# Attention: a new order of each row's work on TensorE, ScalarE and VectorE, group norm folded into two weights, and one head's key halves added on VectorE

## The reference, cut to what matters

```
xn = scale * x + shift                    # group norm, per channel: [256, 128]
q = (xn @ Wq) / sqrt(32);  k = kv_x @ Wk;  v = kv_x @ Wv      # 4 heads of 32
a = softmax(q @ k.T + mask_bias + tri_bias)                   # per head [256, 256]
o = (a @ v) * sigmoid(xn @ Wg)
x1 = x + o @ Wo
```

## Time and profile before

| | us |
|---|---|
| median of 3 runs (lowest, highest) | 4975.86 (4973.19, 4984.57) |
| span of the profiled execution | 4971.8 |
| attention stage, from the first weights issued to the last store issued | 100 to 1981 |

### The profile page before, as it was taken

How to read it: one execution, slowest core, us unless ns; L and a number is a source line. 1 busy time by engine, 2 the same in 40 slices (tenths; PEclk the granted TensorE clock), 3 DMA queues, 4 the chain that set the end, 5 groups by cost and what they waited for, 6 DMA issues and landing times. The chain is left out here.

```text
span 4971.8 us, 107498 instructions
## 1 busy us (share of the span) xinstructions
PE 4518.9 (91%) x35750; PEld 3363.9 (68%) x35750; DVE 3425.0 (69%) x10052; ACT 2805.4 (56%) x6302; POOL 2637.7 (53%) x2043
## 2 busy tenths in 40 slices
PE   6999999999999998858999989997859979999996
PEld 5777777777777776526777757775424438988995
DVE  7888888888888887614666656665259964555555
ACT  0888888888888887013333333333326643555555
POOL 0999999999999998002333313332025530222222
PEclk8999999999999999968999989998879989999997
DMA  7222222222222222984222122222859889999995
GB/s 303 66 74 74 74 75 76 74 74 74 75 76 74 75 74 62 378 304 154 68 68 68 61 89 69 68 69 74 330 199 280 275 261 325 332 328 331 334 338 148
DMA packets 826466, 789.30 MB, mean 159 GB/s; under 512 B 62741, under 2 KB 702740, under 8 KB 817367
## 3 DMA queue, kind: packets, MB, share of 16 engines
q1 hardware_dynamic: 803307, 740.64, 47.5%
q10 hardware_dynamic: 18813, 28.40, 1.6%
q0 software_dynamic: 3808, 13.47, 0.7%
HBM read 574.59 MB, written 207.68 MB: 157 GB/s over the span
## 5 line engine op out<-in xcount | busy, mean ns | idle before, releaser
L309 POOL TENSOR_TENSOR at_bias<-at_tri,at_mask 128x1024 f32<-128x1024 f32 x512 | 1216.4, 2376 | 25.5 <-DMA at_mask<-in_L_conv_mask_bias_dram 10.7
L427 ACT ACTIVATE at_probs<-at_neg_s,at_neg_max 128x256 f32<-128x256 f32 x2048 | 871.0, 505 | 0.7 <-DVE at_neg_max L478 0.7
L478 DVE CUSTOM_DVE_ANT_0 at_neg_s<-at_p_s,at_bias 128x256 f32<-128x256 f32 x2048 | 759.9, 418 | 7.6 <-PE at_p_s L350 2.9
L301 POOL TENSOR_TENSOR at_paired_t<-at_probs_t 128x512 f32<-128x512 f32 x512 | 657.0, 1283 | 9.7 <-ACT at_probs_t L419 5.6
L361 PE MATMUL at_p_t<-all_ident,at_probs 128*128 128x128 f32 x4096 | 628.2, 276 | 0.6 <-DVE at_probs_t L486 0.4
L946 ACT ACTIVATE ml_h<-ml_p,l_b 128x512 f32<-128x512 f32 x384 | 263.9, 687 | 555.6 <-PE ml_p L905 555.6
L1797 PE MATMUL dw_p_conv<-dw_xw,dw_wts 128*128 128x128 f32 x4096 | 512.5, 278 | 68.1 <-issue 46.1
L361 PEld LDWEIGHTS at_p_t<-all_ident,at_probs 128*128 128x128 f32 x4096 | 476.0, 141 | 131.7 <-issue 104.2
L1965 POOL TENSOR_TENSOR dw_xr<-dw_xr,all_b_plain 128x512 f32<-128x512 f32 x128 | 198.1, 1548 | 674.4 <-DMA dw_xr<-x3t 674.4
L1047 POOL TENSOR_TENSOR ml_x2t<-ml_z,ml_xb 128x512 f32<-128x512 f32 x128 | 163.4, 1277 | 735.4 <-DVE ml_z L1013 735.4
L1797 PEld LDWEIGHTS dw_p_conv<-dw_xw,dw_wts 128*128 128x128 f32 x4096 | 483.9, 192 | 85.8 <-issue 84.8
(11 more groups left out here) (225 smaller groups left out, 8921.9 us busy)
## 6 DMA issues: line engine op xcount, KB each, us to landing
dw_wts<-patch_w SPq DMA_DIRECT2D x256, 512.0 KB, 7.3
dw_xw<-planes SPq DMA_DIRECT2D x128, 528.0 KB, 6.0
sp_xs<-x SPq DMA_DIRECT2D x128, 512.0 KB, 8.9
planes<-pw_plane SPq DMA_DIRECT2D x128, 264.0 KB, 3.2
in_xs<-in_x_dram SPq DMA_DIRECT2D x32, 1024.0 KB, 7.7
at_xs<-in_x_dram SPq DMA_DIRECT2D x256, 128.0 KB, 2.5
at_kvs<-in_L_conv_kv_x_dram SPq DMA_DIRECT2D x256, 128.0 KB, 2.7
at_mask<-in_L_conv_mask_bias_dram SPq DMA_DIRECT2D x256, 128.0 KB, 3.3
```

The source lines that it names most:

```text
L301: pool.tensor_tensor(paired_t[:, n % 2, part], probs_t[:, n % 3, part, 0], probs_t[:, n % 3, part, 1], ALU.add).then_inc(paired, 1)
L309: pool.tensor_tensor(bias[:, n % 2, part], tri[:, part], mask[:, n % 4].unsqueeze(1).broadcast_to((128, 4, COLS)), ALU.add).then_inc(maske ...
L427: e = act.activation(probs[:, h, qh, :], neg_s[:, n % 2, h, qh, :], ACT.Exp, bias=neg_max[:, n % 2, i:i + 1], scale=-1.0)
L478: t = dve.tensor_tensor_reduce(neg_s[:, n % 2, h, qh, :], p_s[h][:, qh, :], bias[:, n % 2, i, :], -1.0, 3.0e38, ALU.add, ALU.min, neg_max[ ...
```

## The change

Per image row, the change

1. reorders TensorE's turn: `turn_probs(n,0)`, `score(n+1)`, `weigh(n-2)`, `turn(n+2)`, `turn_probs(n,1)`, `turn_probs(n,2)`, `project_qk(n+2)`, `project_out(n-2)`, `turn_probs(n,3)`, `project_vg(n+2)`, and the lists of ScalarE and VectorE with it;
2. copies both halves of `p_in` with one VectorE copy (`turned_in`), without scale and shift. The scale is multiplied into Wq and Wg once at the start (`wq_n`, `wg_n`); the shift's share becomes a column (`from_shift`) that ScalarE adds as bias when it reads queries and gate;
3. adds head 0's two key halves on VectorE, straight from `p_t[0]` (`pair_first`). GpSimd's first `pair` is left with head 1 alone, half its elements. `turn_probs(n,2)` and `weigh` wait for `paired_first`.

The same amount of TensorE work is done per row, and the DMAs are the same.

```diff
@@ -219,8 +219,11 @@
...
         kvs = m.sb("kvs", [128, 8, HALVES, CH])
-        xn = m.sb("xn", [128, COLS])
-        kvt = m.sb("kvt", [128, COLS])
+        turned_in = m.sb("turned_in", [128, 2, COLS])
+        xt, kvt = turned_in[:, 0, :], turned_in[:, 1, :]
+        wq_n = m.sb("wq_n", [128, CH])
+        wg_n = m.sb("wg_n", [128, CH])
+        from_shift = m.sb("from_shift", [128, 2])
         queries = m.sb("queries", [128, 2, COLS])
@@ -248,6 +251,8 @@
...
         p_turned, even_read, odd_read, paired = (m.sem(n) for n in ("p_turned", "even_read", "odd_read", "paired"))
+        paired_first, scaled, shift_made, shift_read = (
+            m.sem(n) for n in ("paired_first", "scaled", "shift_made", "shift_read"))
         weighed, den_made, den_step, gated = (m.sem(n) for n in ("weighed", "den_made", "den_step", "gated"))
@@ -293,11 +298,12 @@
...
             def pair(n, half):
-                pool.wait_ge(even_read, 2 * n + half + 1)
+                if half:
+                    pool.wait_ge(even_read, 2 * n + 2)
                 pool.wait_ge(odd_read, 2 * n + half + 1)
...
                     pool.wait_ge(weighed, n - 1)
-                part = slice(2 * half, 2 * half + 2)
+                part = slice(2, 4) if half else slice(1, 2)
                 pool.tensor_tensor(paired_t[:, n % 2, part], probs_t[:, n % 3, part, 0], probs_t[:, n % 3, part, 1],
@@ -330,15 +336,15 @@
...
                 pe.wait_ge(turn_read, n + 1)
-                pe.matmul(p_in[:, 0, :], wq_s, xn[:, :], start=True, stop=True)
-                pe.matmul(p_in[:, 1, :], wk_s, kvt[:, :], start=True, stop=True).then_inc(qk_made, 1)
+                pe.matmul(p_in[:, 0, :], wq_n[:, :], xt, start=True, stop=True)
+                pe.matmul(p_in[:, 1, :], wk_s, kvt, start=True, stop=True).then_inc(qk_made, 1)
 
...
                               wv_s, start=True, stop=True)
-                pe.matmul(p_in[:, 1, :], wg_s, xn[:, :], start=True, stop=True).then_inc(vg_made, 1)
+                pe.matmul(p_in[:, 1, :], wg_n[:, :], xt, start=True, stop=True).then_inc(vg_made, 1)
 
@@ -356,6 +362,8 @@
...
                     pe.wait_ge((even_read, odd_read)[h % 2], n * 2 + h // 2)
+                if h == 2:
+                    pe.wait_ge(paired_first, n + 1)
                 for kh in range(HALVES):
@@ -386,27 +395,30 @@
...
             pe.wait_ge(cleared, 1)
+            pe.matmul(p_out[:, 0, 0:1], wq_s, shift, start=True, stop=True)
+            pe.matmul(p_out[:, 0, 1:2], wg_s, shift, start=True, stop=True).then_inc(shift_made, 1)
+            pe.wait_ge(scaled, 1)
+            pe.wait_ge(shift_read, 2)
             for n in range(-2, rows + 2):
+                if exists(n):
+                    turn_probs(n, 0)
                 if exists(n + 1):
-                    project_vg(n + 1)
+                    score(n + 1)
                 if exists(n - 2):
                     weigh(n - 2)
-                if exists(n):
-                    turn_probs(n, 0)
                 if exists(n + 2):
...
                     turn_probs(n, 1)
-                if exists(n + 1):
-                    score(n + 1)
+                    turn_probs(n, 2)
                 if exists(n + 2):
                     project_qk(n + 2)
-                if exists(n):
-                    turn_probs(n, 2)
                 if exists(n - 2):
...
                     turn_probs(n, 3)
+                if exists(n + 2):
+                    project_vg(n + 2)
 
@@ -438,7 +450,8 @@
...
                     act.wait_ge(scored, (n - 1) * HEADS)
-                act.activation(queries[:, n % 2], p_in[:, 0, :], ACT.Copy, scale=float(HEAD_DIM) ** -0.5)
+                act.activation(queries[:, n % 2], p_in[:, 0, :], ACT.Identity, scale=float(HEAD_DIM) ** -0.5,
+                               bias=from_shift[:, 0:1])
                 act.activation(keys[:, n % 2], p_in[:, 1, :], ACT.Copy).then_inc(qk_read, 1)
@@ -446,15 +459,17 @@
...
                 act.activation(vs[:, n % 4], p_in[:, 0, :], ACT.Copy)
-                act.activation(gate_e[:, n % 4], p_in[:, 1, :], ACT.Exp, scale=-1.0).then_inc(vg_read, 1)
+                act.activation(gate_e[:, n % 4], p_in[:, 1, :], ACT.Exp, scale=-1.0,
+                               bias=from_shift[:, 1:2]).then_inc(vg_read, 1)
 
...
                 if exists(n):
-                    exps(n, 1)
                     exps(n, 2)
                     exps(n, 3)
+                if exists(n + 1):
+                    exps(n + 1, 0)
                 if exists(n - 2):
@@ -462,7 +477,7 @@
...
                 if exists(n + 1):
-                    exps(n + 1, 0)
+                    exps(n + 1, 1)
                 if exists(n):
@@ -485,6 +500,13 @@
...
 
+            def pair_first(n):
+                if n >= 2:
+                    dve.wait_ge(weighed, n - 1)
+                dve.wait_ge(even_read, 2 * n + 1)
+                dve.tensor_tensor(paired_t[:, n % 2, 0], p_t[0][:, 0, :], probs_t[:, n % 3, 0, 1],
+                                  ALU.add).then_inc(paired_first, 1)
+
             def denominator(n):
@@ -508,29 +530,35 @@
...
                 dve.wait_ge(turned, n + 1)
-                dve.tensor_scalar(xn[:, :], p_in[:, 0, :], scale, shift, ALU.mult, ALU.add)
-                dve.tensor_copy(kvt[:, :], p_in[:, 1, :]).then_inc(turn_read, 1)
-
+                dve.tensor_copy(turned_in[:, :, :], p_in[:, :, :]).then_inc(turn_read, 1)
+
+            dve.wait_ge(const_loaded, 16 * 6)
+            dve.tensor_scalar(wq_n[:, :], wq_s, scale, None, ALU.mult)
+            dve.tensor_scalar(wg_n[:, :], wg_s, scale, None, ALU.mult).then_inc(scaled, 1)
+            dve.wait_ge(shift_made, 1)
+            dve.tensor_scalar(from_shift[:, 0:1], p_out[:, 0, 0:1], float(HEAD_DIM) ** -0.5, None, ALU.mult).then_inc(shift_read, 1)
+            dve.tensor_scalar(from_shift[:, 1:2], p_out[:, 0, 1:2], -1.0, None, ALU.mult).then_inc(shift_read, 1)
             for n in range(-2, rows + 2):
+                if exists(n):
+                    read_probs(n, 0)
+                    pair_first(n)
+                if exists(n + 1):
+                    add_bias(n + 1, 0)
+                    add_bias(n + 1, 1)
                 if exists(n - 2):
                     denominator(n - 2)
-                if exists(n):
-                    read_probs(n, 0)
                 if exists(n + 2):
...
                     gate(n - 2)
-                if exists(n + 1):
-                    add_bias(n + 1, 0)
-                    add_bias(n + 1, 1)
-                if exists(n - 2):
-                    residual(n - 2)
                 if exists(n + 1):
...
                     add_bias(n + 1, 3)
+                if exists(n - 2):
+                    residual(n - 2)
```

## The result

The changed kernel takes 5411.1 us against 4980.2 (medians of four runs each): 1.086 times the time of before, 95% interval 1.085 to 1.087. Forecast were 5031 us, with 5080 us as the upper end of the range. Executions over 1.5 per cent longer than the fastest of the same kernel, most of them at a lower granted clock, are left out of all medians and ratios here. The span of the changed kernel's profiled execution is 5412.8 us, 441 more than before's 4971.8.

What follows compares the result with a forecast made beforehand. TensorE was taken as the bound, at 7.23 us a row. Saving 0.20 gave 7.03, two waits of 0.18 and 0.23 made 7.44; over 256 rows +54 us, with the start +55: 5031 us, range 4935 to 5080.

Steps and rivals of the forecast that it cites:

- Is VectorE there in time for the copy?: VectorE's work before copying the turned input: denominator done by 3.6 to 3.8 us, turn ends at 3.69; fits by a tenth.
- The third rival: VectorE late for the turned input's copy, by `pair_first`'s wait on its own copy and four full-length additions: 0.2 us more, chance 0.12.
- TensorE's own time: TensorE's row without waits: three changes of bands instead of four save 0.20 us, giving 7.03 us, between 6.81 and 7.14.
- the second rival: The step from scores to values on TensorE costs no drain while both waits stay: 7.22 us a row, about 4975; chance 0.12.
- The chain through `p_in`: TensorE waits for reads of `p_in`: 0.18 us lost between `turn` and `project_qk`, about 0.23 between `project_qk` and `project_vg`.
- One sign: Expected trace evidence on TensorE: weight loads gap over 0.2 us before L333's successor, released by VectorE's `turned_in`.
- The first rival: TensorE is not held at the two `p_in` waits: 7.03 us a row, -51 us, 4925 us; chance 0.19.
- The bias column: ScalarE's reads of queries and gate with a bias column take 0.09 us more each.
- GpSimd: 256 elements take about 0.74 us; GpSimd needs 6.63 us a row and can't stop a row of 7.03 or more.
- The sign: Direction of the whole change: slower, chance 0.69, against 0.22 for faster and 0.09 for same.

Runs made afterwards that it cites:

- the third buffer: Changed kernel with a third buffer of `paired_t`, so `pair_first` and GpSimd's `pair` wait for `weigh(n-3)`, against the kernel before: 5026.2 us, ratio 1.010.
- the other banks: Changed kernel with three `paired_t` buffers, queries, values and gate projected into `p_s` banks, turned input copied in two halves, against the kernel before: 4931.2 us, ratio 0.989.
- Four more kernels: Three `paired_t` buffers with `turn_probs(n,2)` behind `project_qk` (7.65) or without bias column (7.34); kernel before with new orders alone (7.52); the other banks with one copy (7.21).
- `pair_first` alone: Kernel before with only head 0's addition moved to VectorE, old order and two `paired_t` buffers, against the kernel before: 5035.3 us, ratio 1.016, 7.44 us a row.

## Why the prediction was wrong

**The step that failed** is in the part "Is VectorE there in time for the copy?" It has "`pair_first`, which waits for that copy's end, to about 1.80", and then "The new waits for `paired_first` cost nothing: [...] and `weigh` asks for that of two rows back." Both sentences look at who waits for `pair_first`. What `pair_first` itself waits for was left out: the buffer of `paired_t`, hence `weigh(n-2)`. By the prediction's own walk the sums end 3.10 us after the start of `turn_probs(n,0)`, so the addition could not start before 3.1, four bias additions, the denominator and the copy follow, and the copy starts near 5.2 instead of 3.73. The walk's margin of a tenth was looked for in durations, while the wait that decided was not on its list. Measured from `turn_probs(n,1)`, L339's load came at 2.42 instead of 0.95: 1.47 us a row. 7.44 + 1.47 = 8.91, the measured row. So 1.47 x 256 = 376 us of the 380 between forecast and result are this one wait and its queue; the third buffer, which removes only the wait, took away 385. The rest of the sum held: 7.44 us a row forecast, 7.43 measured once the wait is gone.

**The third rival** (VectorE late for the copy) had the right place and the wrong size, 0.2 us for 1.47, since it looked for the delay in durations and not in a wait.

**TensorE's own time** was right: 7.03 us, seen bare with the other banks. The switch from row bands to column bands takes 1.08 us from the scores' start, as the one to the full array took 1.07, and the values' load starts 0.07 us before the scores' recorded end (1006.89 to 1006.96), so the second rival (no drain) is out. The rule of the Trainium skill weighed there (TensorEngine Tiling (Array Packing), Key Properties: changing the mode drains) agrees with that 1.08 us.

**The chain through `p_in`** was right in both places: loads at 0.94 and 1.97 us with the third buffer, for 0.95 and 1.97 forecast. Four more kernels (7.65, 7.34, 7.52 and 7.21 us) came out within 0.01 us of such a count, made before each of them ran, though after the result of the changed kernel. One sign was wrongly put: a gap of over 0.2 us in the weight loads before L333's successor. With the third buffer the transposes' loads end at 1006.29 and L339's starts at 1006.44, a gap of 0.15, which the waits view lists in only 2 rows; TensorE counts as busy all the time there and still loses 0.18 us. The first rival (TensorE isn't held there) is out.

**The bias column** was right: queries take 0.47 us (1003.50 to 1003.97 in the changed kernel's timeline of ScalarE), the 0.38 of the earlier trace rows and the 0.09 of the earlier trace rows, and 0.09 us a row came back without it.

**GpSimd** was right: 729 ns for 256 elements (forecast 740), and no bound.

**The sign** was right for the reasons given, beside the missed one. Even with the wait repaired the change is 1 per cent slower, as the forecast of 5031 said (5026 measured); the part of it that saves time, three changes of bands instead of four, needed the chain cut to show: 0.20 us a row, 48 us between the medians.

## What to carry to other kernels

When an order written out by hand is changed, list for each instruction that moves, and for each new one, what it waits for, buffer guards included, and where the releaser now stands in its own engine's list. A guard that was always met can become the wait that sets the loop's pace; what it costs is not the instruction but the queue behind it, and one more buffer may take it away. A single buffer that is written and read several times in a row of work is a chain with latencies of its own: count the work between its links before and after, and see whether a bank that stands idle at that time can take one of them.

## What the runs showed of the hardware that was not expected

An instruction of VectorE that waits for the one before it on the same engine starts 0.10 us after that one's end (1003.30 to 1003.40), while instructions without such a wait start about 0.08 us before it (1006.07 behind 1005.73 + 0.42, with the other banks). So one addition of 0.42 us, put behind its own copy, moved the copies of the turned input back: they start 1.13 us after the start of the copy of head 0's transposes (1002.87 to 1004.00, `pair_first` alone), where it had been 0.61 (1007.09 to 1007.70 in the timeline of before). That is 0.52 us for the one instruction, not the 0.35 to 0.45 of the expectation; less the 0.3 that the expectation took as covered, it leaves the 0.2 us a row that was measured.
